# Keys of half the heads made eight slots later, behind the output projection, in a cross-attention kernel on one core

## The reference, cut to what matters

```python
def reference(x, ctx, g_xattn, g_ffn, w_q, b_q, w_k, b_k, w_v, b_v, w_o, b_o, w_f, b_f):
    a = layernorm(x)
    q, k, v = a @ w_q.T + b_q, ctx @ w_k.T + b_k, ctx @ w_v.T + b_v      # split in 16 heads
    probs = softmax(causal(q @ k.T / sqrt(32)))
    x = x + tanh(g_xattn) * ((probs @ v) @ w_o.T + b_o)
    y = mx_fp6(layernorm(x))                # values on a 6-bit grid, one scale for 32 features
    return x + tanh(g_ffn) * (y @ mx_fp6(w_f).T + b_f)
```

## Time and profile before

| what | value |
|---|---|
| runs | 1390.13, 1390.96, 1393.0 us (median 1390.96) |
| the profiled execution | 1392.38 us, of which its span (first to last instruction) is 1390.6 us |
| PE busy | 1354.2 us, 97% of the span |
| DVE, POOL, ACT busy | 1124.7, 938.7, 916.6 us |
| DMAs issued by SP for the two stacks | 1536 of 64 KB each |
| median from issue to landing of one of them | 2.0 to 2.1 us |

### The profile page before, as it was taken

The page is one execution under the profiler, slowest core; times in us unless marked ns, Lnnn a source line. Parts: engine busy times, 40 slices in busy tenths (PEclk is TensorE's granted clock), DMA queues, the critical chain, the costliest instruction groups (busy, mean ns, idle before and its releaser), DMA issues.

```text
span 1390.6 us, 34895 instructions
## 1 busy us (share of the span) xinstructions
PE 1354.2 (97%) x10608; PEld 1198.5 (86%) x10608; DVE 1124.7 (81%) x4219; ACT 916.6 (66%) x2969; POOL 938.7 (68%) x1449
## 2 busy tenths in 40 slices
PE   7899999999999999999999999999999999999987
PEld 7788888898888888888888888888888889889865
DVE  5768888788888888888878878888888888888773
ACT  4667666667666666667666667666666666766661
POOL 1657776677676777676677676677677667767564
PEclk9999999999999999999999999999999999999998
DMA  8444344444444444434444434444444444443320
GB/s 253 118 112 107 103 111 124 118 129 107 109 109 120 124 128 117 107 101 119 121 126 123 108 99 115 126 119 124 110 106 109 126 118 128 110 116 99 88 62 31
DMA packets 181912, 159.10 MB, mean 114 GB/s; under 512 B 30176, under 2 KB 164320, under 8 KB 181728
## 3 DMA queue, kind: packets, MB, share of 16 engines
q1 hardware_dynamic: 181728, 156.88, 43.3%
HBM read 39.33 MB, written 16.78 MB: 40 GB/s over the span
## 4 chain that ended last, share of the span: by engine, by line
PE 59%; DVE 20%; SPq 9%; issue 5%; DMA 3%; ACT 1%; POOL 1%; DVEq 0%; ACTq 0%; POOLq 0%
PE proj L549 14%; PE proj L551 13%; PE proj L550 13%; SPq L380 9%; PE pT_ps L616 8%; DVE all_probs L891 5%; PE proj L632 3%; DMA k_stack<-k_lo 3%; DVE stats L899 3%; PE s_ps L605 3%; PE proj L660 2%; DVE all_probs L1028 2%; DVE k_lo L920 2%; PE s_ps L606 1%; DVE oT_lo L954 1%
## 5 line engine op out<-in xcount | busy, mean ns | idle before, releaser
L458 POOL TENSOR_TENSOR all_probs<-all_probs,rden 128x128 f32<-128x128 f32 (+1 forms) x1024 | 504.1, 514 | 347.5 <-DVE rden L949 346.5
L735 ACT ACTIVATE all_probs<-all_probs,neg_max 128x128 f32<-128x128 f32 (+1 forms) x1024 | 458.3, 449 | 242.4 <-DVE neg_max L891 242.2
L891 DVE CUSTOM_DVE_ANT_0 all_probs<-s_ps,causal 128x128 f32<-128x128 f32 (+1 forms) x1024 | 324.4, 354 | 144.2 <-PE s_ps L606 137.1
L616 PE MATMUL pT_ps<-ident,all_probs 128*128 128x128 f32 x1536 | 265.0, 282 | 9.9 <-POOL all_probs L458 7.2
L735 ACT ACTIVATION_READ_ACCUMULATOR all_probs<-all_probs,neg_max 128x1 f32 x1024 | 193.1, 189 | 0.0
L817 ACT ACTIVATE all_probs<-pT_ps 128x384 f32<-128x384 f32 x256 | 125.4, 490 | 87.4 <-PE pT_ps L616 87.2
L616 PEld LDWEIGHTS pT_ps<-ident,all_probs 128*128 128x128 f32 x1536 | 160.8, 142 | 25.2 <-issue 14.1
L549 PE MATMUL proj<-cT_hi,wk_hi 128*128 128x256 f32 x512 | 153.8, 300 | 1.4 <-DVE wk_lo L844 1.4
L605 PE MATMUL s_ps<-k_stack,q_stack 96*128 96x256 f32 x512 | 152.8, 299 | 2.1 <-DVE neg_max L891 2.0
L549 PE MATMUL proj<-aT_hi,wq_hi 128*128 128x256 f32 x512 | 151.0, 295 | 2.3 <-DVE aT_lo L943 2.3
L550 PE MATMUL proj<-cT_lo,wk_hi 128*128 128x256 f32 x512 | 142.7, 279 | 0.0
(11 more groups left out here) (119 smaller groups left out, 3607.9 us busy)
## 6 DMA issues: line engine op xcount, KB each, us to landing
k_stack<-k_hi SPq DMA_DIRECT2D x512, 64.0 KB, 2.0
q_stack<-q_hi SPq DMA_DIRECT2D x512, 64.0 KB, 2.1
xs_yz<-in_x SPq DMA_DIRECT2D x32, 512.0 KB, 5.2
k_stack<-k_lo SPq DMA_DIRECT2D x256, 64.0 KB, 2.0
q_stack<-q_lo SPq DMA_DIRECT2D x256, 64.0 KB, 2.1
out<-xs_yz SPq DMA_DIRECT2D x64, 256.0 KB, 2.3
c_quads<-in_ctx SPq DMA_DIRECT2D x124, 128.0 KB, 2.9
vs<-in_L_xattn_w_k SPq DMA_DIRECT2D x2, 512.0 KB, 5.8
```

The source lines that it names most:

```text
L458: last = nc.gpsimd.tensor_tensor(p, p, rden[:, sd, t, h:h + 1].to_broadcast([P, (1 + t) * P]), ALU.mult)
L616: last = nc.tensor.transpose(pT_ps[h % 2][:, m * P:(m + 1) * P], probs[:, h % P_RING, m * P:(m + 1) * P], ident[:, :])
L735: last = nc.scalar.activation(probs[:, h % P_RING, cols], probs[:, h % P_RING, cols], ACT.Exp, scale=-1.0, bias=neg_max[:, sd, t, h:h + 1] ...
L891: last = nc.vector.tensor_tensor_reduce(probs[:, h % P_RING, cols], s_ps[h % 2][:, cols], causal[:, (1 - t) * P:], 1.0, MASKED, ALU.add, A ...
```

## The change

Each slot now names the parts that it holds (`SLOT_WORK`), with a table of its own for step 1 (`SLOT_WORK_1`); `LAGS` holds the lags. `k0` of batch `i - 1` lies in slots 10 and 11, behind `o` and not ahead of `f`; `q0` in slot 12, `v0` in 13 and 14, `k1` in 14 and 15, and `v1` of batch `i - 2` in slots 1 and 2. The two `xT` stand together in slot 7. In step 1 `k0` stays in slots 1 and 2. SP issues the context loads and the load of `x` ahead of the stack of `k1`, and waits for `left["k"]` ahead of every stack of `k0`. The turns are in slots 3 and 5, both tiles of `xn` in slot 1, `deviation_in` in slot 15. Sixteen more transposes of the identity matrix stand ahead of the first weight's.

```diff
-UNITS = [("q", 1, 2), ("dT", 0, 4), ("k", 0, 1), ("dT", 1, 4), ("f", 0, 4), ("xT", 0, 1), ("f", 1, 4), ("xT", 1, 1),
-         ("o", 0, 3), ("o", 1, 3), ("q", 0, 1), ("v", 0, 1), ("k", 1, 1), ("v", 1, 1)]
+LAGS = {("q", 0): 1, ("q", 1): 2, ("k", 0): 1, ("k", 1): 1, ("v", 0): 1, ("v", 1): 2, ("o", 0): 3, ("o", 1): 3,
...
-WAKING = 12
+WAKING = (12, 16)
...
-XN_SLOTS = (1, 3)
+XN_SLOT = 1
-TURN_SLOTS = (5, 8)
+TURN_SLOTS = (3, 5)
...
             def step(i, ph):
-                if live(i - 2):
-                    if some(n := HEADS * (i - 2)):
-                        sp.wait_ge(max_ok, n)
-                    sp.wait_ge(left["k"], 2 * (i - 2) + 2)
-                    stack("k", i - 2, 1)
                 if at(i, 0):
                     load_first()
...
                     sp.dma_start(xs[:, place(ph, 0), :, :], batch_of(x, i)).then_inc(x_in, 16)
+                if live(i - 2):
+                    if some(n := HEADS * (i - 2)):
+                        sp.wait_ge(max_ok, n)
+                    sp.wait_ge(left["k"], 2 * (i - 2) + 2)
+                    stack("k", i - 2, 1)
...
                         sp.wait_ge(max_ok, HEADS * (b - 1) + HEADS // 2)
-                    else:
-                        sp.wait_ge(left["k"], 2 * b + 1)
+                    sp.wait_ge(left["k"], 2 * b + 1)
                     stack("k", b, 0)
...
-                    if s == 0 and i > 1 and live(i - 1):
-                        deviation_in(i - 1)
+                    if s == LN1_SLOT + 1 and i != 1 and live(i):
+                        deviation_in(i)
...
+                if u == 0:
+                    for _ in range(WAKING[1]):
+                        nc.tensor.transpose(proj[BANKS - 1][:, 0:P], ident[:, :], ident[:, :])
```

More of the change, by code:

```diff
@@ L52 @@
 AV_STEPS = (2, 3)
-UNITS = [("q", 1, 2), ("dT", 0, 4), ("k", 0, 1), ("dT", 1, 4), ("f", 0, 4), ("xT", 0, 1), ("f", 1, 4), ("xT", 1, 1),
-         ("o", 0, 3), ("o", 1, 3), ("q", 0, 1), ("v", 0, 1), ("k", 1, 1), ("v", 1, 1)]
+LAGS = {("q", 0): 1, ("q", 1): 2, ("k", 0): 1, ("k", 1): 1, ("v", 0): 1, ("v", 1): 2, ("o", 0): 3, ("o", 1): 3,
+        ("f", 0): 4, ("f", 1): 4, ("dT", 0): 4, ("dT", 1): 4, ("xT", 0): 1, ("xT", 1): 1}
+SLOT_WORK = ("q1 q1 q1", "dT0 q1 v1", "v1 v1 v1", "dT1", "f0 f0 f0", "f0 f1 f1", "f1 f1", "xT0 xT1 o0 o0", "o0 o0 o1",
+             "o1 o1 o1", "k0 k0 k0", "k0", "q0 q0 q0 q0", "v0 v0 v0", "v0 k1 k1", "k1 k1")
+SLOT_WORK_1 = ("", "k0 k0 k0", "k0", "", "", "xT0", "xT1", "", "", "q0", "q0 q0 q0", "v0", "v0 v0 v0", "k1 k1 k1", "k1", "")
 LAST_O = ((1, ("dT", 0)), (4, ("dT", 1)), (4, ("o", 0)), (5, ("o", 1)), (9, ("f", 0)), (10, ("f", 1)))
 BANKS = 4
-WAKING = 12
+WAKING = (12, 16)
 PARTS = {"cT": 1, "xT": 1, "dT": 1, "q": 4, "k": 4, "v": 4, "o": 4, "f": 4}
-SLOT_PARTS = (3, 3, 3, 1, 3, 4, 3, 3, 3, 3, 3, 1, 3, 3, 3, 2)
 WEIGHT_SLOTS = {"k": (1, (0, 0, 0, 0)), "q": (1, (4, 4, 4, 4)), "v": (1, (6, 9, 9, 9)), "o": (1, (10, 12, 12, 13)),
@@ L99, in live, with units_of @@
         return not isinstance(b, int) or 0 <= b < B
[L101 to L104, removed]
+    def units_of(slot_work):
+        return [(s, (name[:-1], int(name[-1]))) for s, names in enumerate(slot_work) for name in names.split()]
+    assert all(sum(unit == u for _, u in units_of(SLOT_WORK)) == PARTS[unit[0]] for unit in LAGS)
     work = {}
@@ L111, in fused_kernel @@
             for s, (kind, half) in LAST_O:
-                work.setdefault((i, s), []).extend((kind, half, i - lag_of[kind, half], p) for p in range(PARTS[kind]))
+                work.setdefault((i, s), []).extend((kind, half, i - LAGS[kind, half], p) for p in range(PARTS[kind]))
         else:
[L114 to L117, removed]
+            part_of = dict.fromkeys(LAGS, 0)
+            for s, unit in units_of(SLOT_WORK_1 if i == 1 else SLOT_WORK):
+                if live(i - LAGS[unit]):
+                    work.setdefault((i, s), []).append((*unit, i - LAGS[unit], part_of[unit]))
+                part_of[unit] += 1
     work[1, 0] = [("cT", half, 0, 0) for half in range(T)] + work.get((1, 0), [])
@@ L526, in step @@
                         nc.gpsimd.tensor_tensor(xb, xb, add_o[:, :], ALU.add).then_inc(xb_ok, 1)
-                    if i == 0 and s == LN1_SLOT + 1:
-                        deviation_in(0)
-                    if s == 0 and i > 1 and live(i - 1):
-                        deviation_in(i - 1)
+                    if s == LN1_SLOT + 1 and i != 1 and live(i):
+                        deviation_in(i)
+                    if i == 2 and s == 0:
+                        deviation_in(1)
                     for ago, stage in ((1, deviation), (4, scaled), (7, dequantised), (8, with_bias)):
@@ L541, in _ @@
             pe.wait_ge(ident_ok, 1)
-            for _ in range(WAKING):
+            for _ in range(WAKING[0]):
                 nc.tensor.transpose(proj[BANKS - 1][:, 0:P], ident[:, :], ident[:, :])
@@ L1028, in step @@
                         nc.vector.tensor_copy(probsT[:, h % AV_HEADS, :], pT_ps[0][:, 0:3 * P]).then_inc(pT_even, 1)
-                    if s in XN_SLOTS and i > 1 and live(i - 1):
-                        normal_rows(i - 1, XN_SLOTS.index(s))
+                    if s == XN_SLOT and i > 1 and live(i - 1):
+                        for t in range(T):
+                            normal_rows(i - 1, t)
                     for r in range(2):
```

## The result

| | before | after |
|---|---|---|
| median | 1390.55 us (1389.67 to 1393.0, 4 runs) | 1620.49 us (1615.3 to 1620.81, 4 runs) |
| ratio | | 1.164, 95% interval 1.161 to 1.167 |
| span of the profiled execution | 1390.6 us | 1618.4 us |
| mean granted clock of PE | 0.989 | 0.927 |

The change made the kernel 16% slower; 1585 us was forecast, with a range of 1535 to 1640.

The account below looks back on a forecast made before the run. PE's work was taken as the bound, 40.97 us a step; plus 5.3 wait and 1.5 clock gives 47.8, +194 us over 30 steps. 1392.4 + 194 - 1.5 + 1, less 1.4, is 1585 us, range 1535 to 1640.

Parts of the forecast that it names:

- What bounds the kernel, and the wait removed: PE's work sets a 40.97 us step floor; `k_hi`'s wait for `k1`'s stack goes, and with it 10.6 us in all.
- The chain from `k_lo` to head 0: From slot 12, `k_lo`, twelve `k0` DMAs and six of `q0` take 15.7 us; PE waits 5.3 us every step.
- The clock: After the idle at head 0, PE runs at 1.2 GHz in slots 0 and 1, costing 1.5 us a step.
- The sum: Steps of 47.8 us add 194 us over 30 steps; with fill, last batch and median corrections, 1585 us.
- the ends: Outside the 30 steps: fill with sixteen transposes -1.5 us, step 2 evens out, `v1` of the last batch +1.
- Edits costed at nothing: Loads' place, turns, `xn` and `deviation_in`: nothing, with a bound of 0.3 us a step should DVE be late.
- No wait at head 0: Rival: eighteen issues and a landing fit in 8.0 us, at 0.33 us an issue or less; 1379 us, chance 0.04.
- The wait without the clock: Rival: PE waits at head 0 but no 1.2 GHz follows; 46.3 us a step, 1540 us, chance 0.10.
- A second wait at head 8: Rival: slow issues exceed the 2 us left, PE stops again by up to 2 us a step; 1645 us, chance 0.07.
- `k1`'s new wait for `k0`'s copy: `k_hi` in slot 0 waits until `k0`'s stack lands; covered by PE's wait at head 0, else up to 1.5 us a step.

Follow-up runs that it names:

- experiment 10: Kernel before, with `k1`'s stack issuing eight `k_hi` copies first and four `k_lo` last, waited for separately, plus sixteen fill transposes: 1378.03 us, ratio 0.991.
- experiment 7: Kernel before, with only SP's order changed: context loads and load of `x` ahead of `k1`'s stack: 1423.62 us, ratio 1.025.
- experiment 2: Changed kernel with `k0` three slots earlier, in slots 7 and 8 ahead of `o`, `q0` where it was: 1440.65 us, ratio 1.037.
- experiment 3: Changed kernel with four more DMAs of 32 KB between `k0`'s and `q0`'s stacks in every step but the first: 1696.97 us, ratio 1.221.
- experiment 4: Changed kernel with SP's DMAs reordered: six of `k0`, six of `q0`, then the other six of each: 1563.22 us, ratio 1.124.
- experiment 5: Changed kernel with 40 transposes of the identity on PE ahead of head 0's wait, from the second batch on: 1574.12 us, ratio 1.132.
- experiment 9: Kernel before, with only the sixteen extra transposes of the identity in the fill: 1388.43 us, ratio 0.9990.
- experiment 1: Kernel before, with only the new table of slots and lags and SP's new wait for `k0`: 1613.87 us, ratio 1.161.
- experiment 8: Kernel before, with only turns in slots 3 and 5, both `xn` in slot 1 and `deviation_in` in slot 15: 1464.75 us, ratio 1.052.

## Why the prediction was right

- **What bounds the kernel, and the wait removed.** Right in the place, and nearly in the size. I counted 10.6 us by a floor of 40.97 us for each of 30 steps; step 3 has no `f` work and took less than that floor, and the other 29 steps were 11.4 us above theirs, of which experiment 10 gets back 11.0. The copy of `k1` being too close to `k0` as its cause is shown by experiment 10 from one side and by experiment 7 from the other.
- **The chain from `k_lo` to head 0.** Right, and the reason for the loss: forecast 2.4 + 8.0 + 3.2 + 2.1 = 15.7 us, measured 2.60 + 8.04 + 3.25 + 2.10 = 15.98; forecast wait 5.3 us, measured 15.98 - 10.36 = 5.6, where 10.36 is slots 12 to 15 without a wait. `k_lo` ends 2.51 us behind the start of its slot, `q_lo` before 2.64: of the 0.86 us of the `q_lo` that left slot 11 DVE won 0.13. Shown by experiments 2 (fewer issues ahead of `q0`: gone), 3 (four more: +2.5 us a step) and 4 (another order: head 0's and head 2's waits near those worked out).
- **The clock.** The mechanism was right, and this is the term that was mis-sized: 1.5 us a step forecast, but slots 0 and 1 take 7.1 us where the floor of 40.97 leaves 5.0 for them, so 2.1. It fits the trace: the granted clock was 0.50 for 4.4 us of slots 0 to 2, where I had taken 3.4 us with a part of it in the idle time. That the clock is the cause is shown by experiment 5. The term gave 45 us; with 2.1 it gives 63.
- **The sum.** A step takes 41.0 + 5.6 + 2.1 = 48.7 us, where 47.8 was forecast; over 30 steps 221.5 us more than before, not 194. Nearly all the rest of the miss of 35 us lies at the ends: step 3 begins 2.75 us later than before and what follows step 33's head 0 takes 3.5 us longer, where I had -0.5 in all. In that last piece slot 0 alone takes 4.80 us, not 2.58: the last wait's slow clock, which I did not count. Where the 2.75 us of the fill come from, in spite of the 1.7 us that experiment 9 won, is open: step 3 begins 0.4 us later than before with the slots alone (experiment 1) and 2.0 later with the turns, `xn` and `deviation_in` alone (experiment 8), each in one execution.
- **Edits costed at nothing.** Right in the changed kernel: experiment 1 has all but 7 us of the result without them. This is not only because the wait at head 0 hides them. Experiment 2 has them all and almost no such wait, and its 42.9 us a step are the floor of 40.97, 0.8 by which head 0 comes later and 1.0 for `dT0`, which leaves under 0.2. But the loads' place costs 33 us and the turns, `xn` and `deviation_in` 73 where they stand alone (experiments 7 and 8), so the sentence that they move short operations on engines with room was not a sufficient reason. What covers them is the order of the loads, the landing of context and the place of `k0` together.
- **The rivals.** *No wait at head 0* needed 0.33 us an issue; SP took 0.64, and 0.62 for the smaller ones of experiment 3. *The wait without the clock*, 1540 us, did not come by itself; experiment 5, which keeps PE busy, has 1574 us, 46 less. *A second wait at head 8*: slot 7 takes 2.79 us in every step from 4 on, no wait; its first six DMAs landed in time. `k1`'s new wait for `k0`'s copy is there, 29.3 us in all, under the wait at head 0, as it was put.

## What to carry to other kernels

Moving a producer later is free only as far as the queue between it and its reader is free: count the issues that stand ahead of the reader's own, each with its time, and set them against the work left before the reader. Here eighteen issues at 0.64 us and a landing of 2.1 us stood between a unit and its reader, with 10.4 us of PE's work to cover them. And before work is moved to get out of a wait, look at what the wait is for: splitting it in two, for the part that each engine needs, gave 11.0 of the 11.4 us with every unit where it was.

## What the runs showed of the hardware that was not expected

A DMA of 32 KB took SP as long to issue as one of 64 KB (0.62 against 0.64 us). PE's granted clock was 0.50 behind the idle stretch of about 5.5 us in every step of the changed kernel, but also, in 21 of 29 steps, behind two of 1.6 and 2.6 us on average (experiment 4), and in 12 of 29 at or behind a single one of 1.8 to 2.6 us (experiment 8; the 17 others had 2.7 us or less, and one of them none). Two stretches of 0.6 and 1.0 us a step left it at full speed in all 29 (experiment 2). The slow clock after a wait cost more than a third of the wait itself: 2.1 us for 5.6.
